# Cross-attention and MLP block on one core: the context's values computed transposed and turned back, and the second tile's scores and masks ahead of them

## The reference, cut to what matters

```python
xq = layer_norm(x, qn_w, qn_b)
ctx = layer_norm(context, cn_w, cn_b)
q = (xq @ q_w).reshape(B, N, H, D)
kv = (ctx @ kv_w).reshape(B, M, 2, H, D)
k, v = (kv[:, :, 0], kv[:, :, 1])
attn = jnp.einsum('bnhd,bmhd->bhnm', q, k) * scale
attn = jnp.where(xa_mask[:, None, :, :], neg, attn)
attn = jax.nn.softmax(attn, axis=-1)
out = jnp.einsum('bhnm,bmhd->bnhd', attn, v).reshape(B, N, C)
out = out @ proj_w + proj_b
x = x + out
h = layer_norm(x, n2_w, n2_b)
h = jax.nn.gelu(h @ fc1_w + fc1_b, approximate=False) @ fc2_w + fc2_b
return x + h
```

## Time and profile before

| | |
|---|---|
| median of 3 runs | 1050.99 us (1050.1 to 1051.4) |
| the profiled execution, its own time | 1051.01 us |
| span of its trace | 1049.1 us |
| PE busy | 1031.5 us (98% of the span) |
| DVE busy | 835.7 us (80%) |
| ACT busy | 434.2 us (41%) |
| POOL busy | 358.5 us (34%) |
| PE's share of the chain that ended last | 86% (DVE 7%) |

### The profile page before, as it was taken

The page is one execution under the profiler, slowest core; times in us unless marked ns, Lnnn a source line. Parts: engine busy times, 40 slices in busy tenths (PEclk is TensorE's granted clock), DMA queues, the critical chain, the costliest instruction groups (busy, mean ns, idle before and its releaser), DMA issues.

```text
span 1049.1 us, 16369 instructions
## 1 busy us (share of the span) xinstructions
PE 1031.5 (98%) x5857; PEld 855.9 (82%) x5857; DVE 835.7 (80%) x1323; ACT 434.2 (41%) x766; POOL 358.5 (34%) x259
## 2 busy tenths in 40 slices
PE   8999999999999999999999999999999999999998
PEld 6788888888888677778778888888888888888887
DVE  7899999999997989888887666687766677666655
ACT  5344344444445466444542334342433352232221
POOL 3466566667787753243404000304000310300000
PEclk9999999999999999999999999999999999999999
DMA  7012132122210284455567634345536343834312
GB/s 267 9 46 71 53 92 71 63 62 90 74 42 22 79 313 171 171 197 199 180 260 268 235 131 176 131 150 211 210 130 232 118 165 125 311 120 172 124 67 81
DMA packets 52791, 149.19 MB, mean 142 GB/s; under 512 B 11313, under 2 KB 19545, under 8 KB 44531
## 3 DMA queue, kind: packets, MB, share of 16 engines
q1 hardware_dynamic: 52139, 147.25, 39.3%
q10 hardware_dynamic: 584, 1.06, 0.3%
HBM read 108.13 MB, written 39.85 MB: 141 GB/s over the span
## 4 chain that ended last, share of the span: by engine, by line
PE 86%; DVE 7%; issue 3%; POOL 2%; DMA 0%; ACT 0%; SPq 0%; DVEq 0%; POOLq 0%; ACTq 0%
PE bank L1800 29%; PE bank L1770 25%; PE bank L1602 8%; PE bank L1646 8%; PE bank L1583 5%; PE bank L1634 4%; PE bank L1615 3%; PE bank L1779 1%; PE bank L1593 1%; DVE gT L1399 1%; DVE acc L1407 1%; DVE hop L1369 1%; DVE hring L1383 1%; PE bank L1565 1%; DVE w1r L1364 1%
## 5 line engine op out<-in xcount | busy, mean ns | idle before, releaser
L1800 PE MATMUL bank<-w2r,gT 128*128 128x512 f32 x1536 | 360.2, 391 | 3.4 <-DVE acc L1407 3.1
L1800 PEld LDWEIGHTS bank<-w2r,gT 128*128 128x128 f32 x1536 | 286.5, 188 | 66.0 <-DVE acc L1407 7.2
L1770 PE MATMUL bank<-hop,w1r 128*128 128x512 f32 x1344 | 311.9, 390 | 1.3 <-POOL w2r L784 1.3
L1770 PEld LDWEIGHTS bank<-hop,w1r 128*128 128x128 f32 x1344 | 251.3, 188 | 54.0 <-issue 2.1
L1407 DVE TENSOR_TENSOR acc<-bank,acc 128x512 f32<-128x512 f32 x256 | 176.2, 690 | 102.4 <-PE bank L1800 97.7
L1394 DVE TENSOR_TENSOR ybuf<-bank,ybuf 128x512 f32<-128x512 f32 x224 | 148.2, 687 | 71.3 <-PE bank L1770 66.7
L1045 ACT ACTIVATE ybuf<-ybuf,cols 128x512 f32<-128x512 f32 x128 | 91.6, 716 | 162.6 <-DVE ybuf L1394 162.6
L1399 DVE TENSOR_TENSOR gT<-ybuf,gT 128x512 fp32r<-128x512 f32 x128 | 103.9, 833 | 0.0
L684 POOL TENSOR_TENSOR S<-S,rsum 128x1232 f32<-128x1232 f32 x32 | 75.3, 2352 | 61.6 <-DVE rsum L1199 61.6
L649 POOL TENSOR_TENSOR hrs<-hve,mhalf 128x1 f32<-128x1 f32 x32 | 18.0, 562 | 221.0 <-DVE hve L1379 221.0
L792 POOL TENSOR_TENSOR acc<-acc,fc2b 128x512 f32<-128x512 f32 x32 | 43.1, 1364 | 119.8 <-DMA acc<-x_scratch 119.7
(11 more groups left out here) (111 smaller groups left out, 1453.6 us busy)
## 6 DMA issues: line engine op xcount, KB each, us to landing
w1r<-w_scratch SPq DMA_DIRECT2D x24, 1792.0 KB, 7.2
w2r<-w_scratch SPq DMA_DIRECT2D x24, 1024.0 KB, 5.1
w_scratch<-w1r SPq DMA_DIRECT2D x8, 1792.0 KB, 6.0
xr<-in_x SPq DMA_DIRECT2D x32, 256.0 KB, 3.0
x_scratch<-xr SPq DMA_DIRECT2D x32, 256.0 KB, 2.0
hring<-x_scratch SPq DMA_DIRECT2D x32, 256.0 KB, 2.9
acc<-x_scratch SPq DMA_DIRECT2D x32, 256.0 KB, 3.9
w_scratch<-w2r SPq DMA_DIRECT2D x8, 1024.0 KB, 9.2
```

Of the source, the lines that this page charges most:

```text
L1770: mm = pe.matmul(bank_[:, :], w1r[:, w1_slot(s), c, w, kk * P:(kk + 1) * P], hop[i][:, d, kk, :], start=(kk == 0 and n == 0), stop=(kk == ...
L1800: mm = pe.matmul(bY[t % 2][:, :], gT[s % 2][:, j, d, t * P:(t + 1) * P], w2r[:, s % 2, j, w, :], start=(n == 0), stop=(n == 5))
```

## The change

In step -1 the values are no longer computed as rows of tokens. `values_T(h2)` computes half of their 512 columns, transposed, for both contexts at once (8 float32 products of 154 columns, the shape in which `keys(h2)` computes the keys), `values_half(h2)` copies that to a new tile `vT`, and `values(b)` is now 4 transposes, from `vT`, into the bank from which `values_out(b)` copies as before. `vT` lies where `S1` lies, the scores of unit 1, which are first written in step 0. The calls are put in another order on PE, ACT and DVE.

```diff
@@ scalar_program @@
+        def values_half(h2):
+            act.wait_ge(t_valT, h2 + 1)
+            act.activation(vT[:, 2 * h2:2 * h2 + 2, :],
+                           bank[6 + h2][:, 0:2 * B * M].rearrange("p (g n) -> p g n", g=2), ACT.Copy).then_inc(a_valT, 1)
+
@@ scalar_program, step, prep == "scores" @@
                 x_hi(0)
                 x_hi(1)
+                values_half(0)
+                values_half(1)
                 exp_all(0)
+                q_hi(0)
                 values_out(0)
-                q_hi(0)
+                values_out(1)
                 exp_all(1)
                 q_hi(1)
-                values_out(1)
@@ vector_program, step, prep == "scores" @@
                 x_lo(1)
-                normed()
                 for g_ in range(KT):
                     masked(1, g_)
                 maximum(1)
                 exp_sum(0)
                 recip(0)
+                normed()
                 q_lo(0)
@@ tensor_program @@
+        def values_T(h2):
+
+            if h2 == 0:
+                pe.wait_ge(d_vw, 16)
+            else:
+                pe.wait_ge(v_qbias, 1)
+            for g_ in (2 * h2, 2 * h2 + 1):
+                for k in range(KT):
+                    i = pe.matmul(bank[6 + h2][:, (g_ % 2) * B * M:(g_ % 2 + 1) * B * M],
+                                  kvw[:, k, C + g_ * P:C + (g_ + 1) * P], cxT[:, k, :, :].rearrange("p b m -> p (b m)"),
+                                  start=(k == 0), stop=(k == KT - 1))
+            i.then_inc(t_valT, 1)
+
         def values(b):
 
-            pe.wait_ge(d_vw, 16)
-            if b == 1:
-                pe.wait_ge(v_qbias, 1)
-            for k in range(KT):
-                i = pe.matmul(bank[6 + b][0:M, :], cxT[:, k, b, :], kvw[:, k, C:2 * C],
-                              start=(k == 0), stop=(k == KT - 1))
+            if b == 0:
+                pe.wait_ge(a_valT, 2)
+            for g_ in range(KT):
+                i = pe.transpose(bank[6 + b][0:M, g_ * P:(g_ + 1) * P], vT[:, g_, b * M:(b + 1) * M], ident[:, :])
             i.then_inc(t_vals, 1)
@@ tensor_program, step, prep == "scores" @@
                 score(0, 2)
                 score(0, 3)
-                values(0)
                 for g_ in range(KT):
                     score(1, g_)
-                for m in range(KT):
-                    q(m)
+                values_T(0)
+                values_T(1)
+                q(0)
+                q(1)
+                values(0)
                 values(1)
+                q(2)
+                q(3)
                 pe.wait_ge(v_wp, KT)
                 return
```

More of the change, by code:

```diff
@@ L175, in build_block @@
     S = [S0, S1]
+    vT = at("vT", [P, KT, B * M], F32, offset=S1_at)
     bnst = at("bnst", [P, UT, 6], F32)
@@ L254, in build_block @@
     t_keys, a_keys, v_keys, t_vals, a_vals = (sem(n) for n in ("t_keys", "a_keys", "v_keys", "t_vals", "a_vals"))
+    t_valT, a_valT = sem("t_valT"), sem("a_valT")
     t_qbias, v_qbias, v_wscale, a_wq, v_wq, a_wp, v_wp = (sem(n) for n in ("t_qbias", "v_qbias", "v_wscale", "a_wq",
```

## The result

The changed kernel takes 1053.95 us in the median of 14 runs (1052.4 to 1057.79), the kernel before 1051.05 us in the median of 14 (1049.92 to 1055.41). The ratio is 1.0029, with a 95% interval of 1.0017 to 1.0042: slower by about 3 us, and 1053.95 lies beyond the 1052.3 at which the predicted range ended. The profiled execution took 1052.76 us, 1.75 us more than that of the kernel before; its span is 1050.9 us.

What follows compares the result with a forecast made beforehand. PE was taken as busy 98% of the span, with step 0's start held by DVE's `q_lo(1)`. PE's saving is swallowed there; starting 0.27 us later, taken as 0.3, on 1051.01 gives 1051.3 us, range 1050.1 to 1052.3.

Steps and rivals of the forecast that it cites:

- PE's start of step 0: First score of step 0, held by DVE's `q_lo(1)`: forecast at 47.06 us against 46.79, 0.27 us later.
- its saving: PE in step -1 has 1.61 us less to do, all lost in the wait for `q_lo(1)`.
- PE's new work: PE in step -1: 16 products for the transposed values, 4.38 us, and 8 transposes, 0.87 us, replacing 6.86 us.
- ACT's chain: ACT in step -1: `exp_all(1)` behind both `values_out` copies, starting at 43.20 us, 0.24 us later than before.
- `exp_all(0)`: ACT in step -1: starts at about 39.0 us instead of 36.88, behind the two copies to `vT`.
- Rival A: PE's saving goes through: step 0 starts at 45.1 us, 1.7 us earlier, time 1049.3 us; chance 0.07.
- Rival B: In step 0, `av(0)` waits 0.8 us for the cut values, time 1052.1 us; chance 0.12.
- SP's first transfer of context 0: SP's cutting of the values starts at 42.92 us; they arrive at about 54.1, hidden with 1.4 us of slack.
- the term for `normed()`: DVE path ahead of `exp_sum(1)`: two normalizations priced at 1.88 us, leaving DVE free at 44.5 us.
- PE's new gap: PE idle some 1.9 us ahead of step 0, with no cost to the clock in the sum.
- rival C: PE's clock falls to half behind the new gap, costing 3.0 us, time 1054.3 us; chance 0.05.
- The argument against C: A gap of 0.98 us ahead of the transposes at 31.06 us left the following scores at their pace.

Runs made afterwards that it cites:

- e_scores_first: Kernel before with the second tile's scores and mask additions ahead, normalization behind the reciprocal, POOL's `probs(0)` waiting for it, values computed as before: 1050.79 us, ratio 0.9996.
- e_pool_waits: Changed kernel with POOL holding `probs(0)` until DVE's normalizations of unit 2 are written: 1054.44 us, ratio 1.0026 to the kernel before.
- e_normed_back: Changed kernel with DVE's two normalizations back ahead of the second tile's mask additions: 1054.42 us, ratio 1.0015 to the kernel before.
- e_gap_before: Kernel before with two more DVE reductions, results unused, ahead of `recip(1)`, so that PE stands still before step 0: 1055.20 us, ratio 1.0032.
- e_fill_large: Changed kernel with three products of 512 columns, results unread, behind `q(3)` to fill PE's gap: 1053.27 us, ratio 1.0013 to the kernel before.
- e_late_large: Changed kernel, `probs(0)` waiting for the normalization, context 1's transposes and copy behind `q(3)` and `q_hi(1)`, two large filling products: 1050.43 us, ratio 0.9992.
- e_fill: Changed kernel with nine small identity products, results unread, behind `q(3)` to fill PE's gap: 1056.80 us, ratio 1.0046 to the kernel before.
- c_before: The kernel before, unchanged, run again beside itself: 1050.45 us, ratio 0.9989.
- e_late_second: Changed kernel, `probs(0)` waiting for the normalization, context 1's transposes and copy behind `q(3)` and `q_hi(1)`, four small filling products: 1053.44 us, ratio 1.0009.

## Why the prediction was wrong

**What held.** PE's start of step 0 is set by `q_lo(1)`, and its saving is swallowed there; in e_scores_first, where PE's own work sets it, the start came only 0.2 us earlier than in the kernel before. PE's new work, by distances of starts, was 4.10 and 0.80 us, for 4.38 and 0.87; ACT's chain came to 43.06 against 43.20; `exp_all(0)` came 0.2 earlier than forecast, because the first copy to `vT` ran at 36.40 already. Rival A, that the saving goes through, did not come. Rival B did not either: SP's first transfer of context 0 went out at 42.77 (42.92), and `av(0)` had no wait.

**The first step that failed, in the sum,** is the term for `normed()` in the path over DVE: "`normed()`, 1.88". It was read from the earlier trace rows as if it were the work of two instructions. It was one instruction of about 0.5 us and one that waited for POOL's `less_max(0)` to end; in the changed kernel the second one met the beginning of `probs(0)` and waited for nearly all of its 2.4 us. That is 0.98 us more; 0.2 of it was covered by `exp_sum(0)` being early, and 0.77 is the miss of step 0's start. e_pool_waits shows it: 0.92 us with POOL still, and the way to step 0 shorter by 0.83. The page "SBUF — State Buffer" of the Trainium skill, in its terms, says that DVE and GpSimd arbitrate for a shared pair of ports, exclusively and for a whole instruction; the trace agrees, since the second instruction ended 0.3 us behind POOL's and took five times its usual time; and `probs(0)`, which began beside the first one, took 2.41 us where POOL's other ones here took 2.25. The price with POOL still stood in DVE's timeline of the kernel before, and I did not use it: two of the same instructions in 1.00 us, with nothing on POOL:

```profile
21.97 1.00 DVE L1216 TENSOR_SCALAR xhat<-xr,mv,rstd 128x512 f32<-128x512 f32 x2
```

**The second step that failed, and the larger one in time,** is that the sum put PE's new gap at no cost to the clock and left that to rival C with a chance of 0.05. With the `normed()` term right the forecast would still have failed: e_normed_back and e_pool_waits have nearly the start and the gap that were forecast, and are 2.4 and 3.3 us over before. C's mechanism was right, and its price of 3.0 us was too large for one time: it happened behind the gap in two traces of four, at about 1.35 us each, and in the mean the changed kernel has some 1.9 us less of full clock. That a gap of 0.98 us left the clock alone said little about one of 1.9, let alone of the 2.75 that came. The argument against C was also misread from too short a stretch. The new gap was not "twice as long as any" at the full level, and PE does not run "without a gap" from step 0 on: the kernel before has waits of 1.56 us at 362 and 1.32 us at 536, at a granted clock of 1.00.

```profile
362.26 0.65 PE L1615 MATMUL bank<-ident,S 128*128 128x128 f32 x4 [1.56 <-POOL S L684]
```

e_gap_before shows the gap as the cause without the change. In e_fill_large the clock is higher with the gap filled, and in e_late_large, without a gap or a new wait, it is that of the kernel before (0.9993 and 0.9991).

**The sum as it came:** 1.02 us late start, 1.9 us of clock (give or take 1), 0.2 us open: 3.1. The timelines show less of it directly: 1.02 us in all four, 0.7 in the mean for the clock at the gap, and 0.3 in the mean for the longer wait at 538 us, 2.0 in all. The other 1.1 us lie within the scatter of the means or elsewhere, and that stays open: there are one to four traces of a kernel, and two of them, those of e_normed_back and e_fill, have a low stretch later, from 537 and from 712 us on, behind waits of 1.90 and 2.19 us.

## What to carry to other kernels

A group's duration is not its work: before an instruction is moved, ask what else ran on the engine it shares a port with, and price it both with and without. The shortest, middle and longest of its instructions in the whole trace show at once if there are two prices. And work taken from PE where PE waits for another engine anyway becomes a gap: nothing is gained, and if the gap is longer than those that the trace already shows to be harmless, it may cost clock as well. Keep cover behind the last product that the next step waits for, or fill it with work that is not needed.

## What the hardware showed that was not expected

- A DVE normalization of 128x512 float32 took 0.46 to 0.55 us beside an idle POOL and 2.48 us when it was started while POOL ran an elementwise instruction of 2.4 us; the other DVE forms here (`tensor_reduce`, 1.44 us, and additions from a bank) took the same either way.
- The executions of one kernel differ by where PE's clock is low. In the kernel before's first trace 1.2 GHz lasts to 13.6 us and 12 products with the identity at 7.96 take 2.93 us. In c_before the same ones take 1.60 us, as at 2.4 GHz:

```profile
7.90 1.60 PE L1517 MATMUL bank<-ident 128*128 128x128 f32 x12
```

- The number of PE's instructions may matter where its program returns to the start of the loop over the MLP blocks, at 705 us. By the page, the changed kernel has 24 products and transposes more than the kernel before (5881 and 5857), and e_late_large 28 more; neither shows a wait there. With 30 more (e_fill_large) the wait was 1.91 us, with 32 (e_late_second) 2.17, with 42 (e_fill) 2.23 and 2.19 us. That is what five kernels show together; it was not tested by itself. The page "Runtime: NRT & Kernel Launch" of the Trainium skill, under "Instruction fetch mechanics", says that a taken branch breaks the sequential prefetch of instructions and may wait for a fetch; two of the rows put the wait down to "issue", which fits.
